# The second attention of a four-layer kernel: TensorE's order written out group by group, with three probability buffers and four score banks

## What is computed

```
xn = _layernorm(x)
qkv = xn @ W_attn + b_attn
q, k, v = jnp.split(qkv, 3, axis=-1)          # each to (B, H, T, 8)
att = jnp.einsum('bhtd,bhsd->bhts', q, k) * (1.0 / math.sqrt(D))
att = att + rel_bias                          # bias of head h at distance t - s
att = jnp.where(causal, att, -jnp.inf)
att = jax.nn.softmax(att, axis=-1)
y = jnp.einsum('bhts,bhsd->bhtd', att, v)
out = y.transpose(0, 2, 1, 3).reshape(B, T, C) @ W_proj + b_proj
```

## Time and profile before

| | us |
|---|---|
| median of 3 runs | 1021.46 (1021.34 to 1021.85) |
| the profiled execution: its time | 1021.87 |
| its span (first to last instruction) | 1020.0 |
| PE busy | 893.1 (88%) |
| DVE busy | 802.7 (79%) |
| ACT busy | 616.0 (60%) |

### The profile page before, as it was taken

One profiled execution on the slowest core, in us unless ns is written; L12 is line 12 of the kernel. 1 busy time (PEld: TensorE's weight loads), 2 busy tenths in 40 slices (PEclk: granted clock), 3 DMA queues, 4 the chain that ended last, 5 costly groups with the idle time before them and its releaser, 6 DMA issues. The chain is left out here.

```text
span 1020.0 us, 22162 instructions
## 1 busy us (share of the span) xinstructions
PE 893.1 (88%) x8501; PEld 458.3 (45%) x8501; DVE 802.7 (79%) x1600; ACT 616.0 (60%) x1312; POOL 200.7 (20%) x249
## 2 busy tenths in 40 slices
PE   5689999999999997966499999999998998776788
PEld 3212222222222224864254545554545666655568
DVE  7789999999999952647787787778773587799687
ACT  3228888888888885434136677767773346333652
POOL 2302033341202110540300011102010023133121
PEclk9659999999999998987669999999999998979799
DMA  2632444623426320121633753423301000000001
GB/s 78 188 89 65 116 122 100 118 64 87 119 78 143 119 38 14 52 65 27 197 95 109 196 106 81 95 65 96 72 8 35 1 2 1 1 0 1 4 6 37
DMA packets 61782, 73.72 MB, mean 72 GB/s; under 512 B 20247, under 2 KB 45968, under 8 KB 61662
## 3 DMA queue, kind: packets, MB, share of 16 engines
q1 hardware_dynamic: 47354, 49.22, 20.0%
q0 software_dynamic: 8576, 17.86, 7.1%
q10 hardware_dynamic: 5748, 5.22, 1.6%
HBM read 44.59 MB, written 18.16 MB: 62 GB/s over the span
## 5 line engine op out<-in xcount | busy, mean ns | idle before, releaser
L1042 DVE TENSOR_REDUCE a_negmax<-a_mbank 128x1 f32<-128x1024 f32 (+4 forms) x640 | 491.2, 819 | 68.0 <-PE a_mbank L835 38.7
L997 ACT ACTIVATE a_probs<-a_ebank 128x512 f32<-128x512 f32 (+3 forms) x896 | 434.0, 555 | 125.8 <-PE a_ebank L864 68.9
L827 PE MATMUL a_mbank<-a_moving,a_still 48*128 48x512 bf16 (+4 forms) x1280 | 265.4, 379 | 22.1 <-DVE a_ident L1004 14.2
L855 PE MATMUL a_ebank<-b_moving,b_still 50*128 50x512 bf16 (+4 forms) x1280 | 264.6, 362 | 11.5 <-ACT a_probs L997 9.8
L878 PE MATMUL a_acc<-a_probs,a_slot_v 128*32 128x512 f32 (+3 forms) x1792 | 220.8, 565 | 1.1 <-ACT a_probs L997 1.1
L855 PEld LDWEIGHTS a_ebank<-b_moving,b_still 58*64 58x64 bf16 (+1 forms) x1280 | 85.7, 101 | 247.2 <-ACT a_probs L997 208.0
L827 PEld LDWEIGHTS a_mbank<-a_moving,a_still 56*64 56x64 bf16 (+1 forms) x1280 | 70.4, 104 | 86.7 <-DVE a_negmax L1042 63.0
L864 PE MATMUL a_ebank<-a_bias_b,anti 64*64 64x176 bf16 (+4 forms) x1728 | 89.6, 228 | 0.0
L864 PEld LDWEIGHTS a_ebank<-a_bias_b,anti 64*64 64x64 bf16 x1728 | 70.3, 108 | 8.6 <-issue 0.4
L835 PE MATMUL a_mbank<-bias_a,anti 64*64 64x176 bf16 (+3 forms) x576 | 66.6, 242 | 0.0
L878 PEld LDWEIGHTS a_acc<-a_probs,a_slot_v 128*32 128x32 f32 x1792 | 35.4, 108 | 48.1 <-issue 37.2
(11 more groups left out here) (389 smaller groups left out, 1106.2 us busy)
## 6 DMA issues: line engine op xcount, KB each, us to landing
a_slot_v<-vo SPq DMA_DIRECT2D x16, 512.0 KB
b_moving<-stack SPq DMA_DIRECT2D x64, 96.0 KB
b_still<-stack SPq DMA_DIRECT2D x32, 192.0 KB
a_still<-stack SPq DMA_DIRECT2D x60, 96.0 KB, 2.7
a_moving<-stack SPq DMA_DIRECT2D x60, 96.0 KB, 2.7
expert<-in_expert_rows POOLq DMA_DIRECT2D x8, 578.0 KB, 4.0
a_bias_b<-trow SPq DMA_DIRECT2D x32, 66.0 KB
stack<-expert SPq DMA_DIRECT2D x4, 384.0 KB, 2.9
```

The lines of the kernel that those rows point to most:

```text
L827: last = nc.tensor.matmul(mbank[COLS * c:COLS * (c + 1), bank, lo - left:hi - left], S.a_still[rows, q % 2, pr, at[c]:at[c] + COLS], S.a_m ...
L855: last = nc.tensor.matmul(ebank[COLS * c:COLS * (c + 1), step % NE, lo:512], S.b_still[rows, buf, pr, at:at + COLS], S.b_moving[rows, buf, ...
L997: nc.scalar.activation(probs[:, g % 2, j, lows[g]:512], ebank[:, step % NE, lows[g]:512], ACT.Exp).then_inc(p_full, 1)
L1042: nc.vector.tensor_reduce(to[:, at:at + 1], mbank[:, (index - 1) % NM, 0:right - left], AX.X, ALU.max, negate=True).then_inc(m_empty, 1)
```

## The change

For the second attention the two tables give way to `ORDERS[True]`: three strings of 12 words, for the first, the six middle and the last turn. A word is what TensorE does in a group: `0` to `3` are scores, `u` a unit, `V` the oldest values not yet done, `A` and `B` the turned maxima of the first and second half, `p` a tile of the projection. Only where `01` stands together are scores 0 and 1 laid down alternately. For the first attention the strings spell out the order that it had.

```
-STARTS = {False: [23 + 2 * g for g in range(17)], True: [45, 50, 55, 57, 59, 65, 70, 75, 80, 85, 89, 92, 93]}
-EARLY = [32, 37, 42, 47, 61]
+ORDERS = {
...
+    True: [
+        "01u2u3 uu0uuu12uu3 0uu1uuuuVuuBuuuuuu23 0u1uuu23 uuV012uuuVu3 0u12Vu3 "
+        "uuAV0u1uu2V3 u0u1u2u3 u0u12uuVuu3 u0uu12u3 uVu01u2u3 u01VV2u3uu",
+        "0123 uVVuu0uBu12uu3 0uVuu123 u0u1u2u3 uVu01u23 Vuu0V12u3 "
+        "uAuuVu01u2uu3 uu01u2uV3 u0u12uuVu3 012uuuV3 u012uuuV3 uu01uVu23uu",
+        "0123 0VVB12p3 0V12Vp3 01p23 0p123 p0VV123 "
+        "0V123 V012p3 01pV23 01V23p 0123 V0123VVV",
+    ],
...
-    NM, WIDE = (4, 512) if causal else (2, SEQ)
-    TURN, LATE, LAST = (19, 3, 2) if causal else (18, 2, 1)
+    NM, WIDE = (3, 512) if causal else (2, SEQ)
+    TURN = 19 if causal else 18
+    AHEAD, NPB, COPY = (34, 3, (1, 1)) if causal else (23, 2, (0, 3))
...
-    NE = 3
+    NE = 4 if causal else 3
...
-        probs = sb("probs", [P, 2, QUAD, 512])
+        probs = sb("probs", [P, NPB, QUAD, 512])
...
-            def turn(q):
+            def turn(q, unit, valued, tiles):
...
+                for g, word in enumerate(orders[q]):
+                    for at, c in enumerate(word):
+                        if causal and word[at:at + 2] == "01":
+                            issue(scores(q, g, 0, buf), scores(q, g, 1, buf))
+                        elif causal and c == "1" and word[at - 1:at] == "0":
+                            continue
+                        elif c in "0123":
+                            issue(scores(q, g, int(c), buf))
+                        elif c == "u":
+                            issue(a_use(*divmod(next(unit), USES)))
+                        elif c == "V":
+                            values(next(valued))
+                        elif c == "p":
+                            projected(next(tiles))
+                        else:
+                            turn_maxima(*((q, 1) if c == "B" else (q + 1, 0)))
...
-                act.wait_ge(p_empty, q * G + (end + 3))
+                act.wait_ge(p_empty, q * G + (end + 1 + NPB))
...
-                        if kt == 0 and j == 3 and q + h:
+                        if (kt, j) == COPY and q + h:
```

More of the change, by code:

```diff
@@ L471, in attention_phase @@
     USES = len(units)
-    NM, WIDE = (4, 512) if causal else (2, SEQ)
-    TURN, LATE, LAST = (19, 3, 2) if causal else (18, 2, 1)
+    NM, WIDE = (3, 512) if causal else (2, SEQ)
+    TURN = 19 if causal else 18
+    AHEAD, NPB, COPY = (34, 3, (1, 1)) if causal else (23, 2, (0, 3))
     groups = [(h, kt) for h in range(2) for kt in range(4 * h + 4 if causal else BT)]
     lows = [max(kt * P - 512 * h, 0) if causal else 0 for h, kt in groups]
-    starts = STARTS[causal]
     G = len(groups)
-    opening = EARLY + starts[len(EARLY):] if causal else starts
-    NE = 3
+    NE = 4 if causal else 3
     BQ = HEADS // QUAD
     layer = 1 if causal else 0
-    tiles_from = NQUAD * USES + LAST
-    tile_every = (starts[0] - LAST) // BT
-    turned_at = {q * USES + TURN: (q, 0) for q in range(NQUAD)}
-    turned_at.update({(q + 1) * USES + (LATE if q + 1 < NQUAD else LAST): (q, 1) for q in range(NQUAD)})
-    def span(q, g):
-        at = starts if q else opening
-        n, end = q * USES + at[g], q * USES + at[g + 1]
-        return n, (n + end) // 2, end
-    def place_steps():
-        place, count = {}, itertools.count()
-        def maxima(first, end):
-            for n in range(first, end):
-                if n in turned_at:
-                    place[turned_at[n]] = next(count)
-        maxima(0, opening[0])
-        for q in range(NQUAD):
-            for g in range(G):
-                n, middle, end = span(q, g)
-                place[q, g, 0], place[q, g, 1] = next(count), next(count)
-                maxima(n, middle)
-                place[q, g, 2], place[q, g, 3] = next(count), next(count)
-                maxima(middle, end)
+    orders = [ORDERS[causal][0 if q == 0 else 2 if q + 1 == NQUAD else 1].split() for q in range(NQUAD)]
+    def place_steps():
+        place, count = {(0, 0): 0}, itertools.count(1)
+        for q in range(NQUAD):
+            for g, word in enumerate(orders[q]):
+                for c in word:
+                    if c in "0123":
+                        place[q, g, int(c)] = next(count)
+                    elif c in "AB":
+                        place[(q, 1) if c == "B" else (q + 1, 0)] = next(count)
         return place
@@ L514, in attention_phase @@
     COLS = HALF if causal else P
-    assert G % 2 == 0 and starts[0] < USES + LATE and len(follows) == 2 * NQUAD
+    assert NQUAD * G % NPB == 0 and len(follows) == 2 * NQUAD and all(len(o) == G for o in orders)
     with nc.cleanup_on_exit(), ExitStack() as ctx:
@@ L868, in scores, with values @@
                 last.then_inc(e_full, 1)
-            def values(q, g, buf):
+            def values(k):
+                q, g = divmod(k, G)
+                buf = q % 2
                 h, kt = groups[g]
@@ L910, in previous @@
-            def previous(q, g):
-                if g:
-                    values(q, g - 1, q % 2)
-                elif q:
-                    values(q - 1, G - 1, (q - 1) % 2)
+                for g, word in enumerate(orders[q]):
+                    for at, c in enumerate(word):
[13 more added lines that the diff above has]
+                            turn_maxima(*((q, 1) if c == "B" else (q + 1, 0)))
@@ L946, in _ @@
                     bias_rows(side)
-            issue(first_pass(20 if sort else 0, opening[0]))
+            issue(first_pass(20 if sort else 0, AHEAD))
+            unit, valued, tiles = itertools.count(AHEAD), itertools.count(), itertools.count()
             for q in range(NQUAD):
-                turn(q)
-            values(NQUAD - 1, G - 1, (NQUAD - 1) % 2)
+                turn(q, unit, valued, tiles)
+            assert next(unit) == NQUAD * USES and next(valued) == NQUAD * G and next(tiles) == BT
         @block.scalar
@@ L1033, in quad @@
                 for use, what in enumerate(units):
-                    if use == TURN + 3 and q == BQ + 2:
+                    if use == 21 and q == BQ + 2:
                         invert()
```

40 lines of the change are left out of this document (11 added, 29 removed), and 7 rows, old and new, of the table ORDERS.

## The result

The changed kernel takes 993.48 us (median of 4 runs, 993.28 to 993.98) against 1021.65 us (4 runs, 1021.34 to 1022.61) for the kernel before on the same chip. The ratio is 0.9727, 95% interval 0.9713 to 0.9741. The direction was right.

A forecast was written before the change was run, and what follows sets the result against it. TensorE's program was taken to set the pace. From 1021.87 us, six middle turns take off 5.2 and the last turn 4.4, while opening and first turn add 1.8: 1014.1, stated as 1014 us, range 1008.5 to 1020.5.

The forecast's parts named there:

- the sum of a middle turn: Middle turn: 25.5 us of columns, 3.0 of switches and 2.3 of waits before; 29.9 us forecast after, 0.9 less.
- without any wait the turn takes 29.3 us: Middle turn after the change: columns 26.5 us plus 2.8 us for eleven changes to values.
- the parted pairs: Middle turn: five words part scores 0 and 1, giving up 1.56 us of overlap; units beside them give 0.56 back.
- What I had named as a sign of being wrong: Matmuls on opposite halves not running side by side where a unit stands next to a single score.
- `halves` 1.15: Middle turn: the wait before the turned maxima, called the largest of the waits, 1.15 us, taken as gone.
- I take these as gone too: Waits of scores for a bank, taken as gone with a fourth score bank; one exponential takes 0.54 us.
- The first rival: Three unit banks make TensorE wait for VectorE: middle turn 31.6 us, 0.8 more, 1027 us in all; chance 10%.
- The last turn: First score to last values: 27.2 us instead of 31.6, 4.4 less; bounds 0.5 to 6.5 less.
- The opening: Before the first score: two more units at VectorE's 0.64 us each, 1.3 us more.
- The third rival: First turn's clock moves: staying at 2.4 GHz saves up to 6.8 us, 1008 (10%); low longer, 1019 (8%).
- the forecast's +0.5: Turn 0: 0.5 us longer, from 0.9 more for columns and switches, with 0.4 less waiting for `halves`.

The follow-up runs named there:

- old_maxima_later: The kernel before with the transpose of the second half's maxima (`B`) three units later: 1024.54 us, ratio 0.9995.
- new_banks_4_3: The changed kernel in its new order with the banks of before, 4 for units and 3 for scores: 1023.04 us, ratio 0.9983.
- new_early_values: The changed kernel with every value one group behind, right behind score 2, and the copies of `acc` a group earlier: 1039.24 us, ratio 1.0115.
- old_order_late_values: The kernel before's order with values two groups behind, three probability buffers, four score banks and three unit banks: 1030.39 us, ratio 1.0063.
- old_one_by_one: The kernel before with scores 0 and 1 of the second attention laid down one after the other, not alternately: 1022.76 us, ratio 0.9992.

## Why the prediction was wrong

**The step that failed** is the sum of a middle turn: "Pieces on different halves of the array run side by side when they are neighbours in the order", and what follows from it, "without any wait the turn takes 29.3 us". Two errors grew from it. First, the columns: the parted pairs were charged with +1.0 us, where the halves lose nothing by being apart; by the rule that the runs bear out, columns and switches fall by 0.9. Second, since too much was put down to columns and switches (28.5 of 30.8 us), only 2.3 us were left for waits. There were 6.2 by the estimate above, of which the change took 2.8, more than I thought there was to win. The measured 27.1 us lie below the 29.3 that I had called the turn without any wait, which alone refutes the sum. What I had named as a sign of being wrong was the opposite error, that neighbours might not run side by side; that pieces might do so without being neighbours had no rival and no chance.

**The waits.** The forecast took them one by one from the list: `halves` 1.15, the rest small. Taken away alone, the first was worth 0.3 us a turn (`old_maxima_later`). That a wait is listed at all depends on which half idles: a half that waits beside a busy one shows only as a waiting weight load. Those rows were on the table: 55.0 us in the earlier trace rows, which I dismissed as lying under values, and 30.3 us of VectorE's in the earlier trace rows, which I read only as a risk for the three unit banks. From 560 to 740 us, which lie inside the block in both profiles, the first fell from 50.0 to 23.8 us and the second from 29.8 to 13.2. But a part of the waiting only moved: the weight loads of units waited 5.0 us for VectorE before and 27.2 after. And VectorE's waits follow the length of a turn by arithmetic, since its work in a turn is the same 24.3 us; they show the gain, not its cause.

**The banks.** "I take these as gone too", of the waits for a score bank, was right only in company. The first rival was right on its mechanism: three unit banks, with the fourth score bank in return, cost 1.4 us a turn in the old order and would have sunk the change there. It was wrong that they would in the new one, where the units come one to three at a time.

**The last turn.** Forecast 27.2 us from the first score to the last values; it is 26.0, and was 31.6:

```profile
716.31 0.40 PE L856 MATMUL a_ebank<-b_moving,b_still 58*64 58x512 bf16 x2
...
740.80 1.50 PE L881 MATMUL a_acc<-a_probs,a_slot_v 128*32 128x384 f32 x24
```

The size came within 1.2 us. Its sum stands on the failed rule too, so that this is in part luck and no proof of its parts; that the fourth score bank and the late values bring it fits the runs. From the first exponential, as in the table, it is 29.7 us with the old banks (`new_banks_4_3`), 28.5 with values one behind (`new_early_values`), 28.3 with both in the old order (`old_order_late_values`) and 25.1 in the changed kernel.

**The opening.** +2.95 instead of +1.3; the missing 1.8 is the third unit bank, which I had priced for the middle turns and forgotten where VectorE bounds.

**Turn 0.** The third rival, at 10%, had it: the clock stays up, at most 6.8 us. It gave 4.7. Whether the change or chance kept it up is open (see the end), so this part of the gain may be luck. The count under the forecast's +0.5 was off too: the new first turn parts 0 from 1 in eight words, not six.

**What stays open.** Why the changed order is the one that runs free is shown only from outside: take back any one of three things (the banks, the values' places, the units' places) and the turn is 31 to 32 us again. The lag was only taken back together with the values' places (32.4 us against 31.2 with the places alone), so what it is worth in the changed order isn't shown. What I can only argue is that two loops pass through TensorE, one over the unit banks and VectorE and one over the score banks and ScalarE, and that a delay in either comes round again in the other. I have no sum that gives 27.1 for one order and 31.2 for its neighbour, and the spread of units over the groups, which looked like one, isn't it.

## What to carry to other kernels

Work out TensorE's floor for each row half by itself, joined only at instructions that need all rows; the order between halves is free, and what lies between that floor and the measured time is waiting, even where TensorE is "busy" for 95% of the time. When an order, the number of banks and a lag are tuned together, undoing one at a time doesn't give its share: here each of three held the whole gain, so a part that loses alone (three unit banks and four score banks, +1.4 us a turn) is no reason to reject the whole. And a buffer that is given from one stage to another has a price wherever the first stage is bounded by its reader, here 1.8 us in the opening.

## What the hardware showed that I had not expected

The two row halves of the array each follow their own order. A score's main pieces began ahead of six bias pieces that stand before them in the program (613.02 and 613.13), and putting scores 0 and 1 one behind the other changed the turn by 0.00 us.

The second stretch of low clock in turn 0 doesn't seem to be a property of the program alone. With the same instructions in nearly the same order it was there in one profile (13.6 us of it) and not in another, and it is worth 4.7 us, 0.5% of the kernel. Over the seventeen profiles it is absent in six, and the clock is low for 6.8 to 23.9 us of it in eleven. It isn't bound to turn 0 either: in `old_maxima_later` a stretch of 23.9 us fell into the last turn and made it 9.6 us longer than the same program's in the kernel before. What decides it isn't settled: ahead of it TensorE was busy for 5.6 of 6.8 us in the kernel before, which has it, and for 6.68 of 6.80 us in `old_one_by_one`, which has not; but the changed kernel, which has not either, was busy there for 5.22 of 6.00 us:

```profile
521.00:527.00 6.00, 5.22 (x89) 2.44 (x88) 6.00 (x13) 2.53 (x7) 0.00 (x0) 1.00 0.01 3
```
